# One buffer per unit in the layer normalisation stage, its loops written out, and the first two token lists read in place

## The reference, cut to what matters

```python
def reference(x, w_qkv, w_out, wg, w1, b1, w2, b2):       # x: (8, 1024, 256) float32
    xn = layernorm(x)                                     # per token: (x - mean) / sqrt(var + 1e-5)
    return x + attention(xn, w_qkv, w_out) + moe(xn, wg, w1, b1, w2, b2)

def attention(x, w_qkv, w_out):                           # 16 heads of 64, causal
    q, k, v = split(einsum('bse,ehd->bshd', x, w_qkv), 3)
    p = softmax(where(causal, q @ k.T / 8, very_negative))
    return einsum('bshd,hde->bse', p @ v, w_out)

def moe(x, wg, w1, b1, w2, b2):                           # 8192 tokens, 8 experts, top 2
    scores = softmax(x @ wg)                              # wg: (256, 8)
    topv, topi = top_k(scores, 2); topv /= topv.sum()
    pos = place of each choice in its expert's list (first choices first), at most 2048 per expert
    disp[topi, pos] = x                                   # choices beyond 2048 are dropped
    y = relu(disp @ w1 + b1) @ w2 + b2                    # w1: (8, 256, 1024), w2: (8, 1024, 256)
    return sum over the two choices of topv * y[topi, pos]
```

## Time and profile before

| | us |
|---|---|
| median of 3 runs | 3183.21 |
| the profiled execution's own time | 3178.04 |
| its span (first to last instruction) | 3175.8 |
| TensorE busy in the span | 3040.6 (96%) |
| VectorE busy | 2185.1 (69%) |
| ScalarE busy | 1710.6 (54%) |
| GpSimd busy | 1606.0 (51%) |

### The profile page before, as it was taken

One profiled execution on the slowest core, in us unless ns is written; L12 is line 12 of the kernel. 1 busy time (PEld: TensorE's weight loads), 2 busy tenths in 40 slices (PEclk: granted clock), 3 DMA queues, 4 the chain that ended last, 5 costly groups with the idle time before them and its releaser, 6 DMA issues.

```text
span 3175.8 us, 64704 instructions
## 1 busy us (share of the span) xinstructions
PE 3040.6 (96%) x22707; PEld 2412.5 (76%) x22707; DVE 2185.1 (69%) x5088; ACT 1710.6 (54%) x3866; POOL 1606.0 (51%) x2380
## 2 busy tenths in 40 slices
PE   5599999999999999999999999999999999999998
PEld 3489998999977777777777777777777777777776
DVE  6844444444337777887787787778777777877776
ACT  3454444445435555555555555555555555555554
POOL 2132221222116666666666666666666666666664
PEclk7799999999999999999999999999999999999999
DMA  6122221222113334334333423433342343334222
GB/s 212 34 79 78 72 70 46 75 78 72 59 59 74 82 96 108 74 85 108 91 82 93 111 74 81 112 91 81 91 114 74 79 110 94 77 90 115 71 72 70
DMA packets 204433, 272.60 MB, mean 86 GB/s; under 512 B 61264, under 2 KB 161616, under 8 KB 204128
## 3 DMA queue, kind: packets, MB, share of 16 engines
q1 hardware_dynamic: 179712, 201.94, 23.8%
q0 software_dynamic: 24416, 66.65, 8.0%
HBM read 102.80 MB, written 33.55 MB: 43 GB/s over the span
## 4 chain that ended last, share of the span: by engine, by line
PE 60%; ACT 4%; issue 4%; DVE 2%; SPq 0%; DMA 0%; DVEq 0%; ACTq 0%
PE S L1275 15%; PE O L1312 13%; PE T L1288 10%; PE W L1191 9%; PE S L1191 3%; PE W L1206 3%; PE S L1206 3%; ACT pr L1350 3%; PE W L1226 3%; PE S L1226 2%; ACT pT L1342 1%; DVE pr L1406 1%; SPq L1130 0%; PE S L1214 0%; DMA pT<-squares 0%
## 5 line engine op out<-in xcount | busy, mean ns | idle before, releaser
L1350 ACT ACTIVATE pr<-pr,negm 128x128 f32<-128x128 f32 (+7 forms) x1024 | 787.3, 770 | 670.0 <-DVE negm L1406 665.7
L1551 POOL TENSOR_SCALAR pr<-pr,rinv 128x128 f32<-128x128 f32 (+7 forms) x1024 | 755.5, 745 | 427.4 <-DVE rinv L1412 424.6
L1406 DVE CUSTOM_DVE_ANT_0 pr<-S,late 128x128 f32<-128x128 f32 (+7 forms) x1024 | 730.4, 750 | 40.0 <-PE S L1275 23.7
L1312 PE MATMUL O<-pT,vv 128*64 128x256 f32 (+1 forms) x5120 | 556.1, 364 | 3.1 <-DMA pT<-squares 2.7
L1312 PEld LDWEIGHTS O<-pT,vv 128*64 128x64 f32 x5120 | 346.2, 137 | 205.0 <-issue 45.1
L1288 PE MATMUL T<-ident,pr 128*128 128x128 f32 x2718 | 425.2, 281 | 32.7 <-DVE pT L1342 18.0
L886 DVE TENSOR_TENSOR hl<-h,hh 128x512 fp32r<-128x512 f32 x256 | 190.2, 744 | 323.3 <-ACT hh L847 318.3
L1288 PEld LDWEIGHTS T<-ident,pr 128*128 128x128 f32 x2718 | 297.8, 141 | 140.0 <-issue 118.7
L1342 DVE COPY pT<-T 128x512 f32<-128x512 f32 (+3 forms) x644 | 305.1, 498 | 143.0 <-PE O L1312 111.5
L843 ACT ACTIVATE h<-pH,b1c 128x512 f32<-128x512 f32 x256 | 175.8, 687 | 365.2 <-PE pH L773 353.5
L1275 PE MATMUL S<-kh,qh 64*128 64x512 f32 (+2 forms) x1536 | 317.0, 409 | 6.6 <-DVE negm L1406 6.4
(11 more groups left out here) (193 smaller groups left out, 6590.2 us busy)
## 6 DMA issues: line engine op xcount, KB each, us to landing
pT<-squares SPq DMA_DIRECT2D x756, 128.0 KB
pT<-squares POOLq DMA_DIRECT2D x252, 128.0 KB
y<-yb SPq DMA_DIRECT2D x128, 128.0 KB, 1.7
wr<-in_L_attn_w_qkv SPq DMA_DIRECT2D x128, 128.0 KB, 2.3
x<-in_L_attn_x SPq DMA_DIRECT2D x16, 512.0 KB, 5.3
xn<-xn SPq DMA_DIRECT2D x16, 512.0 KB, 5.2
w1r<-in_L_ffn_w SPq DMA_DIRECT2D x8, 1024.0 KB
w2r<-in_L_ffn_w SPq DMA_DIRECT2D x8, 1024.0 KB
```

What stands on the lines that cost most here:

```text
L1312: ins = e.matmul(O[hs, a:GQ], vv[n // 2 % 2][:, kt, vs], turned_p, start=(kt == 0), stop=(kt == KT - 1))
L1350: e.activation(pr[i][:, 0:w], pr[i][:, 0:w], ACT.Exp, bias=negm[:, i:i + 1], scale=-1.0, accum_out=rsum[:, i:i + 1]).then_inc(expd.sem, 1)
L1406: e.tensor_tensor_reduce(pr[i][:, 0:w], S[s % 2][:, off:off + w], late[:, SEQ - w:], 1.0, -MASKED, ALU.add, ALU.min, negm[:, i:i + 1]).the ...
L1551: e.tensor_scalar(pr[i][:, 0:width(s)], pr[i][:, 0:width(s)], rinv[:, i:i + 1], 1.0, ALU.mult, ALU.mult).then_inc(scaled.sem, 1)
```

## The change

Stage 1: every unit has its own `x4` and `xn4` (16 of each), and `stats`, `mv`, `root` and `rstd` hold all 64 tiles. The loops over rounds are written out. SP issues all 16 loads at the start, then the 16 stores, each as its unit is normalised. The waits for a free `xn4` go away, and so do the waits of `apart`. The orders of TensorE and ScalarE at unit u change as the diff shows. Stage 3: groups 0 and 1 are gathered by row numbers read directly from `slot_token`. The copies into `idx` begin with group 2.

```diff
-        x4 = [sb(f"x4_{i}", [P, UT, MODEL]) for i in range(RING)]
-        xn4 = [sb(f"xn4_{i}", [P, UT, MODEL]) for i in range(RING)]
+        x4 = [sb(f"x4_{u}", [P, UT, MODEL]) for u in range(UNITS)]
+        xn4 = [sb(f"xn4_{u}", [P, UT, MODEL]) for u in range(UNITS)]
...
         @block.sync
         def _(e):
-            e.dma_start(x4[0][:], xv[0]).then_inc(in_[0].sem, 16)
-            for q in range(RING):
-                e.sem_inc(out_[q].sem, 16)
+            e.dma_start(x4[0][:], xv[0]).then_inc(s_in[0], 16)
             e.wait_ge(s_wz, 1)
             e.dma_start(wg_sb[:, :, 0:EXPERTS], wg.rearrange("(c p) n -> p c n", p=P)).then_inc(s_wg, 16)
-            for q in range(1, RING):
-                e.dma_start(x4[q][:], xv[q]).then_inc(in_[q].sem, 16)
...
+            for u in range(1, UNITS):
+                e.dma_start(x4[u][:], xv[u]).then_inc(s_in[u], 16)
+            for u in range(UNITS):
+                e.wait_ge(norm.sem, norm.at(u, 1))
+                e.wait_ge(normp.sem, normp.at(u, 1))
+                e.dma_start(xnv[u], xn4[u][:]).then_inc(s_out, 16)
+            e.wait_ge(s_out, 16 * UNITS)
...
         @block.vector
...
-                for b in range(CU):
-                    q = h * CU + b
-                    if not first:
-
-                        e.wait_ge(out_[q].sem, out_[q].at(n // 2 - 1 if isinstance(n, int) else (n - h) // 2 - 1, 16))
-                        e.wait_ge(tr.sem, tr.at(n * CU + b - RING, 1))
-                    normalise(e, q, DVE_TILES, norm)
...
+            def finish(n):
+                invert(n)
+                for u in range(n * CU, (n + 1) * CU):
+                    normalise(e, u, range(UT - 1), norm)
+
+
+            for u in range(UNITS):
+                statistics(u)
+                if u % CU == 0 and u > 0:
+                    finish(u // CU - 1)
+                aggregate(u)
+            finish(UNITS // CU - 1)
 
         @block.gpsimd
...
+            for u in range(UNITS):
+                e.wait_ge(refine.sem, refine.at(u // CU, 5))
+                normalise(e, u, range(UT - 1, UT), normp)
 
         @block.scalar
...
+            root_of(0)
+            for u in range(UNITS):
+                copy(u)
+                if u >= 2:
+                    keep(u - 2)
+                if u >= 1:
+                    take(u - 1)
+                if u % CU == 0 and u // CU + 1 < UNITS // CU:
+                    root_of(u // CU + 1)
+            keep(UNITS - 2)
+            take(UNITS - 1)
+            keep(UNITS - 1)
 
         @block.tensor
...
+            e.wait_ge(s_wg, 16)
+            for u in range(UNITS):
+                transposes(u)
+                if u >= 2:
+                    turn(u - 2)
+                if u >= 1:
+                    product(u - 1)
+            turn(UNITS - 2)
+            product(UNITS - 1)
+            turn(UNITS - 1)
...
-        staged = Count(sem("s_staged"), 1)
+
+        staged = Count(sem("s_staged"), 1, -2)
...
             def gather(sg, half, q, first=False):
 
+                tokens = slot_token[:, sg * GT:(sg + 1) * GT] if first else idx[q][:]
                 if not first:
                     e.wait_ge(gat[q].sem, gat[q].at(half - 1, 16 * GT))
                     apart(e, s_apart[0])
                     e.wait_ge(tX.sem, tX.at(sg - 2, 1))
                     apart(e, s_apart[0])
-                e.tensor_copy(idx[q][:], slot_token[:, bass.ds(sg * GT, GT)]).then_inc(staged.sem, 1)
-                e.wait_ge(staged.sem, staged.at(sg, 1))
-                apart(e, s_apart[0])
+                    e.tensor_copy(tokens, slot_token[:, bass.ds(sg * GT, GT)]).then_inc(staged.sem, 1)
+                    e.wait_ge(staged.sem, staged.at(sg, 1))
+                    apart(e, s_apart[0])
                 for t in range(GT):
                     e.indirect_dma_start(xg[q][:, t, :], None, xn_dram,
-                                         bass.IndirectOffsetOnAxis(ap=idx[q][:, t:t + 1], axis=0)).then_inc(gat[q].sem, 16)
+                                         bass.IndirectOffsetOnAxis(ap=tokens[:, t:t + 1], axis=0)).then_inc(gat[q].sem, 16)
```

More of the change, by code:

```diff
@@ L172, in _, with statistics, aggregate @@
             e.memset(wg_sb[:], 0.0).then_inc(s_wz, 1)
-            def aggregate(u, q):
-                h, at = q // CU, q % CU * UT
+            def statistics(u):
+                e.wait_ge(s_in[u], 16)
+                for t in range(UT):
+                    ins = e.bn_stats(stats[:, u * UT + t, :], x4[u][:, t, :])
+                ins.then_inc(stat.sem, 1)
+            def aggregate(u):
                 e.wait_ge(stat.sem, stat.at(u, 1))
[L177 to L180, removed]
+                for t in range(u * UT, (u + 1) * UT):
+                    ins = e.bn_aggr(mv[:, t, :], stats[:, t, :])
+                if u % CU == CU - 1:
@@ L244, in _, with root_of @@
             e.wait_ge(s_eps, 1)
-            def sqrt(n, h):
+            def root_of(n):
                 e.wait_ge(aggr.sem, aggr.at(n, 1))
[L248 to L265, removed]
-                    e.wait_ge(tr.sem, tr.at(u, 1))
-                    for h in range(2):
-                        ins = e.activation(xT[b][:, 4 * h:4 * h + 4, :].rearrange("p a b -> p (a b)"), pT[b][:, h, :], ACT.Copy)
-                    ins.then_inc(trc.sem, 1)
-                    if not (first and q == 0):
-                        keep(u - 1, 1 - b)
@@ L273, in _, with copy @@
-            sqrt(0, 0)
-            rounds(e, body, True)
-            take(UNITS - 1, 1)
-            keep(UNITS - 1, 1)
+                e.activation(root[:, of_pair(n)], mv[:, of_pair(n), 1], ACT.Sqrt, bias=eps[:, 0:1]).then_inc(rooted.sem, 1)
+            def copy(u):
+                e.wait_ge(turned.sem, turned.at(u, 1))
+                for h in range(2):
+                    ins = e.activation(xT[u % 2][:, 4 * h:4 * h + 4, :].rearrange("p a b -> p (a b)"), pT[u % 2][:, h, :], ACT.Copy)
+                ins.then_inc(copied.sem, 1)
@@ new lines, in take, with keep @@
+            def take(u):
+                e.wait_ge(multiplied.sem, multiplied.at(u, 1))
+                e.activation(lT[u % 2][:], pL[u % 2][:], ACT.Copy).then_inc(taken.sem, 1)
+            def keep(u):
+                e.wait_ge(back.sem, back.at(u, 1))
+                e.activation(logits[:, u * UT:(u + 1) * UT, :], pG[u % 2][:, :, 0:EXPERTS], ACT.Copy).then_inc(kept.sem, 1)
+            root_of(0)
[7 more added lines that the diff above has]
+                    root_of(u // CU + 1)
@@ L303, in product @@
                                        start=(m == 0), stop=(m == MC - 1))
-                ins.then_inc(lg.sem, 1)
-            def turn(u, b, first):
-                e.wait_ge(lgc.sem, lgc.at(u, 1))
-                if not first:
-                    e.wait_ge(gtc.sem, gtc.at(u - 2, 1))
-                e.transpose(pG[b][:].rearrange("p t c -> p (t c)"), lT[b][:], k["ident"][:]).then_inc(gt.sem, 1)
-            def body(i, first, last):
-                for q in range(RING):
-                    u = i * RING + q
-                    if not (first and q == 0):
-                        product(u - 1, (q + 1) % 2, first and q < 3)
-                    transposes(u, q, first and q < 2)
-                    if not (first and q == 0):
-                        turn(u - 1, (q + 1) % 2, first and q < 3)
```

134 lines of the change are left out of this document (45 added, 89 removed).

## The result

| | before | after |
|---|---|---|
| median of the first 4 runs each | 3182.43 us (3176.19 to 3183.53) | 3161.81 us (3161.28 to 3164.23) |
| ratio after to before | | 0.9941 (95% interval 0.9923 to 0.9958) |
| profiled execution, own time | 3178.04 | 3161.90 |
| span | 3175.8 | 3160.1 |
| stage 1, to the first instruction of stage 2 | 82.5 | 67.6 |

The change gains 20.6 us by the medians and 16.1 us by the two profiled executions. I had forecast 3169.6 us and a range of 3165.5 to 3175.5, so the gain is larger than all of the range allowed.

The account below looks back on a forecast made before the run. VectorE's work and the ring's load pace stage 1; TensorE is busy from 165 us on. Stage 1's 12.4 plus the gather's 1.25 us takes 3178.04 to 3164.4; 5.2 to the median gives 3169.6 us, range 3165.5 to 3175.5.

Parts of the forecast that it names:

- the same difference: Last step: runs' median 3183.21 lies 5.2 us above the profiled execution; added to 3164.4, this gives 3169.6 us.
- The wait of the ring: Stage 1: VectorE's wait for a load of x before the next pair's statistics goes, 1.52 us per pair.
- The loops: Stage 1: writing out the loops takes 0.25 us off VectorE's time per pair, giving a period of 6.89 us.
- The first pair: Stage 1: the first pair is unchanged, its normalisation starting at 13.95 us.
- The tail: End of stage 1: from last normalisation at 61.2 to 69.3 at high clock, 72.9 at low; 69.8 taken, 12.4 us earlier.
- the root would be in time: Stage 1, ScalarE: next pair's root ready at 5.5 us, VectorE asks at 5.84; in time by 0.3 at low clock.
- the low clock: TensorE at 1.2 GHz: last root some 0.8 us later; rival with late root, 3171.5 to 3175.5 us, chance 0.22.
- The gather: Start of stage 3: first two indirect DMAs stay held behind w1l and w2l; dropping the idx copies gains 1.25 us.
- the naive 2.8: Stage 3: full 2.80 us price of the two idx copies, gained if durations were first-use costs; included in forecast's 0.58.
- a stall of the instruction streams: Written-out loops need more fetching, cost nothing to 3 us; within rival "little arrives", 3176 to 3180 us, chance 0.10.
- The last store: End of stage 1: goes out at about 61.2 + 3.3, lands 5.2 us later at 70 to 70.5; nothing added.
- The slower rival: Stage 1: 16 loads share DMA engines, second statistics start 20.7 us later, stage ends at 90.5; 3190 us, chance 0.04.

Follow-up runs that it names:

- gather_alone: The kernel before with only stage 3's gather changed; 3178.04 us, ratio 0.9996 to the kernel before.
- before_again: The kernel before, unchanged, run for another trace; its profiled execution took 3181.63 us.
- after_again: The changed kernel, unchanged, run again as yardstick of the second set; 3162.21 us, ratio 0.9936 to the kernel before.
- ring4: The changed kernel with a ring of four x4 and xn4 buffers instead of sixteen; 3170.19 us, ratio 0.9963 to the kernel before.
- old_orders: The changed kernel with the orders of TensorE and ScalarE as before the change; 3165.09 us, ratio 0.9946 to the kernel before.
- late_low: The changed kernel with w1l computed only after group 0's gather has landed and w2l after group 0's rows; 3159.82 us, ratio 0.9928 to the kernel before.
- ring4_old: The changed kernel with a ring of four buffers and the old TensorE and ScalarE orders; 3173.1 us, ratio 0.9976 to the kernel before.

## Why the prediction was wrong

*The step that failed* is the one that turned the execution's time into that of the runs: "The median of the runs is 3183.21, 5.2 us above that execution; the same difference gives **3169.6 us**." The changed kernel's profiled time, 3161.90, is its median within 0.1, so the difference was not 5.2 us but none. Without it the forecast would have been 3164.4. As far as the runs tell, three things were in the 5.2 us:

- A part that the change takes away. The execution that I worked from had a short stage 1 for its kernel. Its tail ran at clock 1.00 and took 10.6 us; other traces with loops, ring and old orders took 11.9 (gather_alone, 0.85) and 13.2 (before_again, 0.71). In these two stage 2 began 1.8 and 2.9 us later.
- The luck of three runs. The 15 runs of each set have medians of 3180.04 and 3181.71 us, 1.5 to 3.2 below 3183.21. The chip may have a part in that.
- The luck of one execution. In after_again the profiled one took 3165.77 us, 3.6 above its median, while the first one of the changed kernel lay on it.

*The rest of the miss*, 2.5 us, is in the sum itself. Against the execution's own time I forecast 3164.4, and 3161.9 was measured. Stage 1's last instruction ended at 67.29 and not at 69.8: the first pair began 0.6 us earlier than I took, six periods were shorter by 1.0 in all, and the tail was 1.0 shorter.

*The wait of the ring:* right in mechanism and size. 1.52 us per pair was forecast, and the rooms gave 1.53 (8.25 in ring4, 6.72 after). The ring is worth 9.1 to 9.2 us in stage 1, and without it no load is waited for behind the first pair.

*The loops:* mis-sized. I took 0.25 us per pair; they cost VectorE 0.33, and 0.4 to 0.6 with the longer waits for loads that their traces show. The period came out at 6.72 and not 6.89. About half of that gap is the loops. For the other half, the end of a wait gives 0.12 us more than the wait: with nothing to wait for, the statistics start at 51.42 while the aggregation ahead of them is still running. GpSimd's loop cost too: in the last pair it starts its tile 0.07 us after VectorE, where it took 0.42.

*The first pair:* "unchanged", 13.95, was the late end of a variation that is not the change's. It began at 12.7 to 13.6 in all the other traces, of every kernel, as the second or third load lands earlier or later.

*The tail:* I forecast 8.1 us from the last normalisation at the high clock, and 7.65 was measured. I took a further 0.5 for the clock, which this trace didn't need; after_again, at 0.82, took 9.05 in all. But the prediction gives the orders no price of their own. Its chain follows the new orders, and it is they that keep TensorE up: old_orders, with all rooms, pays 3.6 us for the lack of them. That the root would be in time behind more work on ScalarE was right: in the trace of after only the last inversion waits for it, 0.37 us as before. In late_low, which has the same stage 1, it waited 0.81 us there, after transposes at the low clock. That is 0.4 more, where I had put some 0.8 more on the low clock.

*The gather:* right in mechanism and size. 1.25 us was forecast in place of the naive 2.8, and 1.37 measured (9.67 against 11.04 us from `w1l`'s start to the transposes). late_low shows the cause by taking it away. The Trainium skill (SBUF — State Buffer, "Who interferes with whom") says that a VectorE instruction with two SBUF inputs contends with a GpSimd instruction that reads SBUF. The traces agree: 2.53, 1.88 and 2.09 us beside such instructions, 0.94 to 0.97 without.

*The rest:* nothing points to a stall of the instruction streams. The periods are all 6.72 to 6.73 us, and stage 2 takes 67.3 us where it took 67.0. The last store, which I had landing at 70 to 70.5, went out at 62.5 and had landed when stage 2 began at 67.60. Stages 3 and 4 gave nothing back. From the first product of the experts to the end of the span it is 3175.8 - 165.1 = 3010.7 us before and 3160.1 - 149.2 = 3010.9 after. The slower rival (loads sharing the engines) did not happen: the second unit's statistics began at 8.09.

*What adds up, and what doesn't.* Between the traces of before and after, whose tails both ran at clock 1.00, stage 2 starts 82.61 - 67.71 = 14.9 us earlier. The rooms have 9.2 of it (6 x 1.53), writing out 2.5 (6 x 0.42, from 8.67 to 8.25), the tail with the new orders 2.6 and the first pair's chance 0.6. With the gather's 1.4, less 0.3 that stage 2 was longer, that is 16.0 us; the two spans differ by 15.7 and the executions' own times by 16.1. The medians give 19.5 in the second set and 20.6 in the first runs. Taking all traces, stage 2 starts at 84.2 us on average in the three of before and gather_alone and at 67.9 in the three of after, after_again and late_low (67.41); with the gather's that makes 17.7. The 2 to 3 us between stay unassigned. By the ratios they may stand between the loops and their writing out: gather_alone and ring4_old are 0.0020 apart, or 6.4 us, where their traces have stage 2 starting 4.0 apart. That is no more than a hint: a few traces stand against dozens of runs, and the later stages alone vary by 6 us from trace to trace.

## What to carry to other kernels

Before a sum against one profiled execution is moved to a median, ask which part of the difference lies in what the change removes, and which is only the luck of that execution or of a few runs. Where the median of before is off its trace, look at the trace's clock in the stage concerned. When two traces are compared, match the clocks of the stretch first: here 9.9 us became 9.1. A change that "gives room" often carries a new order of instructions with it, and the order is to be priced by itself: follow one engine's list in both orders and see how many units it is behind at the end. And where an instruction takes far longer the first time, look for what another engine runs beside it before calling it a first-use cost.

## What the runs showed of the hardware

A GpSimd indirect DMA or copy that reads its indices from SBUF beside a VectorE `tensor_tensor` with two SBUF inputs was held until that was over, and then took 0.8 to 0.9 us more (0.05 for the copy). The 0.95 us of a free one so became 2.53. Beside a `tensor_tensor` with one of its two inputs in PSUM it stayed at 0.95 (late_low). SP's queue was held for 20.4 us by 15 loads of 512 KB, 1.36 us each on average (0.47 to 2.62), while the DMA engines moved 348 GB/s (trace of after, from 5 to 24 us). The same work of VectorE took 0.33 us per pair longer in a loop with waits by register values than written out (7.17 against 6.84). The granted clock of the same short stretch of the same kernel differed from run to run: 1.00 and 0.71 in the tail of before, 1.00 and 0.82 in that of after.
